# A graph network's kernel: the first layer's own share multiplied out inside the strips that build the adjacency, with the row turns in two banks and another order at the build's end

## The chip, the cores and the metric

The kernel runs on one core of one Trainium2 chip. The metric is the device time of one execution in microseconds (us), lower is better; the kernel before has a median of 1605.82 us over three runs.

## What is computed

The part that matters here is a graph network of five layers on 3125 nodes with 256 channels and 53125 edges. Each layer computes

```python
edge_fea = concatenate([edge_attr[:, 3:] @ ew1[l], edge_attr[:, 0:3] @ ew2[l]])
msg = norm[:, None] * (h[row] + edge_fea)
agg = segment_sum(msg, col)                                   # sum over the edges that end in a node
h = relu(concatenate([h, agg], axis=1) @ mlp_w[l] + mlp_b[l])  # mlp_w[l] is 512 x 256
h = batch_norm(h) over the nodes; relu except after the last layer
```

The first layer's `h` is the layer-normalised input `x`. Since the product with `mlp_w[l]` is over two halves, it splits into `h @ mlp_w[l][:256]`, here called the **own share**, and `agg @ mlp_w[l][256:]`, here called the aggregate's share. After the five layers a mixture-of-experts block follows which the change does not touch.

## The kernel before

**Layout.** `hT` holds `h` transposed, in float32: 128 partitions (channels) x 2 halves x 3125 nodes. Nodes go in 25 tiles of 125 (`NT`, `P`) and in 7 column blocks `COLS` (`NQ`): six of 500 and one of 125. `aggT` is laid out as `hT`. `m` holds the rows of `h` by node, scaled, as two float16 parts. `at` is the adjacency (counts, fp8), 3125 x 3125, so that an aggregate is a dense product of `m` with `at`.

**Aggregation units.** A unit `g` of 0 to 13 is one column block `g // 2` and one channel half `g % 2`. It takes 25 steps (one per source tile) of two matmuls each, then one short matmul for the edge attributes (`attributes`), and then VectorE evicts it to `aggT` (`evict`, line 724). In the first layer units use the PSUM banks 5, 6 and 7 in turn (`FIRST`), so unit `g` waits for the eviction of `g - 3`. All 14 units are 350 steps (`DENSE`).

**The build.** Nothing but the edge list is given, so the first 437 us or so make `at`. Its main loop goes over 63 **strips** `w` of 50 destination nodes. Per strip VectorE makes one-hot tables (lines 1575 to 1582; line 1582 is the last) in one of two buffers (`side = w % 2`), TensorE multiplies them (lines 1817 and 1819, 8 matmuls each), and the buffer is given back. Two strips are a pair `u`: after the odd one TensorE closes the PSUM bank (line 1823), ScalarE copies it out (`encI`, line 1671), VectorE splits it into two groups of nibbles (`low_nibbles`, `high_nibbles`, lines 1545 and 1549, after the strip that is one pair later), and ScalarE writes five tiles of `at` (line 1689). Per ten strips there are also sums of edge attributes: TensorE `turn_sums` (line 1772) in the strips 12, 22, ..., VectorE `attribute_sums` (lines 1561 to 1565) in the next strip, TensorE `turn_rows` (line 1778), ScalarE `rows_out` (line 1664).

**What else runs in the strips.** In strips 0 to 11 TensorE transposes the 25 input tiles (`across`, line 1736) into the four banks 4 to 7 and ScalarE copies each to `hT` (`turned`, line 1644); `across(t)` waits for `turned(t - 4)`. From strip 13 on TensorE also does up to 6 steps of aggregation per strip (`DENSE_W`, line 699), capped by `dense_after` at 50 steps for ten strips, since a block of `at` is complete only every ten strips; the 22nd, 32nd, ... strip has none. 250 steps are done when the loop ends, 100 are left.

**The end of the build.** After strip 62 each engine runs through a list written out by hand, in program order: TensorE turns the last attribute sums and does the 100 steps that are left; VectorE does the nibbles of pairs 30 and 31, both attribute sums, a check sum and the evictions from unit 8 on.

**The first layer's product.** `linear_pe` (line 786) goes over the 7 blocks: 4 matmuls with `hT` (own share) and 4 with `aggT`, all float32, into banks 0 to 3; a profile row counts 2 records for each. ScalarE adds the bias, takes the ReLU and writes `hT` (line 886), and VectorE takes the statistics (`bn_stats`, line 846, then line 849). The next layer starts with 14 matmuls on zeros (line 746), transposes of `hT` (line 680) and its own aggregation (line 690).

The order of the work on each engine is program order, and every wait is a semaphore. The functions and lines that the change touches:

## Time and profile before

| | |
|---|---|
| median of 3 runs (lowest to highest) | 1605.82 us (1603.84 to 1607.27) |
| profiled execution: time / its span | 1611.95 us / 1610.3 us |
| strips 0 to 62 | 170.4 to 438.6 us of the span |
| end of the build | 438.6 to 479.65 us |
| first layer's product | 479.65 to about 522 us |
| busy share of the span, TensorE / VectorE / ScalarE | 88% / 42% / 25% |

The span is the time from the first to the last instruction of the profiled execution. A profile row gives a start, a duration, the engine, the line and the tiles; in square brackets stands the idle time ahead of it on its engine and what ended it.

### The profile page before, as it was taken

To read this page: it belongs to the slowest core of one execution; us is meant where nothing else is said; L and a number is where in the kernel's file an instruction comes from. 1 tells how busy PE (TensorE), PEld (TensorE's weight loads), DVE (VectorE), ACT (ScalarE), POOL (GpSimd) and SP (SyncE) were. 2 spreads that over 40 slices of the span, in tenths; PEclk is the share of its full clock that TensorE was granted. 3 is DMA by queue.
4 is the path that set the end of the run, shared out by engine and by line. 5 is a ranking of instruction groups with operands and counts; after the bars stand their busy time and mean duration, and the time that the engine had idled before them with its cause. 6 is when DMAs were issued, how large, how long until landed. Compare 5 with 4: busy or idle time off the path is not lost.

```text
span 1610.3 us, 25262 instructions
## 1 busy us (share of the span) xinstructions
PE 1421.4 (88%) x9032; PEld 851.9 (53%) x9033; DVE 674.2 (42%) x1562; ACT 399.4 (25%) x1032; POOL 175.5 (11%) x147
## 2 busy tenths in 40 slices
PE   2566589999899999999999999999999873899996
PEld 2555344444444544545445554445445442899995
DVE  7989888887622310122101320023100267333442
ACT  1320354444402400033001420014100240244442
POOL 2000000000000000000000000000000003477774
PEclk9876789999989999999999999999999976999998
DMA  5144000000000000000000000000001383244443
GB/s 124 56 157 161 1 1 2 1 2 1 15 1 0 14 0 1 1 14 0 1 0 1 14 1 0 1 0 15 0 1 46 62 276 96 42 70 69 71 71 44
DMA packets 49545, 57.76 MB, mean 36 GB/s; under 512 B 14320, under 2 KB 41602, under 8 KB 49185
## 3 DMA queue, kind: packets, MB, share of 16 engines
q1 hardware_dynamic: 38688, 41.67, 9.0%
q0 software_dynamic: 10752, 14.69, 5.5%
q8 instruction: 67, 1.10, 0.3%
q14 instruction: 38, 0.30, 0.1%
HBM read 42.36 MB, written 13.99 MB: 35 GB/s over the span
## 4 chain that ended last, share of the span: by engine, by line
PE 80%; DVE 12%; issue 4%; DVEq 2%; ACT 1%; DMA 1%; POOL 1%; SPq 0%; POOLq 0%
PE bank L690 33%; PE bank L786 13%; PE bank L699 10%; PE bank L1214 6%; PE bank L1223 6%; PE bank L1819 3%; DVE ohL L1467 1%; PE bank L680 1%; PE bank L1760 1%; PE bank L705 1%; PE bank L1817 1%; PE bank L1205 1%; PE bank L1180 1%; DVEq L512 1%; PE bank L1742 1%
## 5 line engine op out<-in xcount | busy, mean ns | idle before, releaser
L690 PE MATMUL bank<-at,m 125*128 125x500 fp8e4 (+1 forms) x2800 | 550.9, 351 | 3.5 <-DVE m L647 3.5
L690 PEld LDWEIGHTS bank<-at,m 125*128 125x128 f16 x2800 | 252.4, 97 | 259.8 <-issue 7.1
L724 DVE TENSOR_TENSOR aggT<-bank,dinvB 128x500 f32<-128x500 f32 (+1 forms) x70 | 42.3, 622 | 389.0 <-PE bank L690 355.8
L886 ACT ACTIVATE hT<-bank,prm 128x500 f32<-128x500 f32 (+1 forms) x65 | 42.5, 654 | 569.2 <-PE bank L786 569.2
L699 PE MATMUL bank<-at,m 125*128 125x500 fp8e4 (+1 forms) x700 | 155.4, 376 | 6.8 <-issue 2.5
L935 POOL TENSOR_TENSOR idJ<-idJ,wts 125x1400 f32<-125x1400 f32 x2 | 8.0, 4006 | 1346.0 <-DVE idJ L1093 1346.0
L1214 PEld LDWEIGHTS bank<-xtT,w1c 128*128 128x128 f32 x896 | 111.2, 196 | 2.8
L1214 PE MATMUL bank<-xtT,w1c 128*128 128x128 f32 x896 | 111.4, 279 | 0.0
L786 PE MATMUL bank<-hT,wcur 128*128 128x500 f32 (+1 forms) x280 | 111.1, 539 | 0.0
L786 PE MATMUL bank<-aggT,wcur 128*128 128x500 f32 (+1 forms) x280 | 110.8, 538 | 0.0
L699 PEld LDWEIGHTS bank<-at,m 125*128 125x128 f16 x700 | 63.5, 103 | 83.6 <-issue 33.5
L1223 PE MATMUL bank<-w2s,h1T 128*128 x448 | 106.1, 380 | 0.0
L846 DVE BATCH_NORM_STATS2 zst<-hT 128x6 f32<-128x500 f32 x60 | 40.9, 681 | 153.2 <-ACT hT L886 153.2
L647 DVE SCALAR_TENSOR_TENSOR m<-bank,dinvP,m 125x256 f16<-125x256 f32 x100 | 47.3, 483 | 132.6 <-ACT m L669 132.6
L951 POOL DMA_INDIRECT out_rows<-ytb,rowS x56 | 95.7, 1709 | 53.1 <-issue 23.5
L1689 ACT ACTIVATE at<-encB 125x500 fp8e4<-125x500 uint8 (+1 forms) x96 | 57.5, 599 | 120.7 <-DVE encB L1545 118.1
L1223 PEld LDWEIGHTS bank<-w2s,h1T 128*128 128x128 f32 x448 | 80.8, 190 | 9.2 <-issue 0.2
L786 PEld LDWEIGHTS bank<-aggT,wcur 128*128 128x128 f32 x280 | 50.4, 190 | 55.1 <-issue 55.1
L786 PEld LDWEIGHTS bank<-hT,wcur 128*128 128x128 f32 x280 | 50.1, 190 | 53.4 <-issue 53.2
L1580 DVE TENSOR_TENSOR cnt<-iotaK,nowKD 128x2000 bf16<-128x2000 int16 x63 | 75.2, 1194 | 0.0
L1819 PE MATMUL bank<-cnt,ohS 128*128 128x250 bf16 x504 | 74.3, 293 | 0.0
L1000 ACT ACTIVATE h1T<-bank,b1T 128x128 f32<-128x128 f32 x224 | 64.0, 368 | 25.4 <-issue 20.5
(318 smaller groups left out, 1413.8 us busy)
## 6 DMA issues: line engine op xcount, KB each, us to landing
slrow<-sl_dram SPq DMA_DIRECT2D x26, 512.0 KB, 4.8
...
wraw<-in_L_gnn_mlp_w SPq DMA_DIRECT2D x5, 512.0 KB, 3.5
```

The lines of the kernel that those rows point to most:

```text
L647: dve.scalar_tensor_tensor(m[:, t, 1, :], bank[t % 4][0:P, 0:D], dinvP[:, t:t + 1], m[:, t, 0, :], ALU.mult, ALU.subtract).then_inc(s_lo, 1)
L690: last = pe.matmul(bank[LATER[g % len(LATER)]][:, 0:w], m[:, s, k, h * 128:(h + 1) * 128], at_block(g // H)[:, s, :], start=False, stop=s ...
L699: pe.matmul(bank[FIRST[g % len(FIRST)]][:, 0:w], m[:, s, k, h * 128:(h + 1) * 128], at_block(g // H)[:, s, :], start=s == 0 and k == 0, st ...
L786: last = pe.matmul(bank[2 * (q % 2) + h][:, 0:w], wcur[:, k, h * 128:(h + 1) * 128], rhs, start=k == 0, stop=k == 2 * H - 1)
L886: act.activation(hT[:, h, a:a + w], bank[2 * (q % 2) + h][:, 0:w], ACT.Relu, bias=prm[:, 0, h:h + 1]).then_inc(s_z, 1)
L951: pool.indirect_dma_start(out[:, :], bass.IndirectOffsetOnAxis(ap=rowS[:, j:j + 1], axis=0), ytb[:, j % XB, :], None, compute_op=ALU.add). ...
L1000: last = act.activation(h1T[:, u, k, :], bank[4 + u][:, k * TT:(k + 1) * TT], ACT.Relu, bias=b1T[:, bass.ds(e, 1), k:k + 1].rearrange("p a ...
L1214: last = pe.matmul(bank[4 + u][:, k * TT:(k + 1) * TT], w1c[:, u, h, k * 128:(k + 1) * 128], xtT[:, u, h, :], start=h == 0, stop=h == H - 1)
L1223: last = pe.matmul(bank[6 + u][:, 0:D], h1T[:, u, k, :], w2s[:, bass.ds(e, 1), k, :].rearrange("p a f -> p (a f)"), start=k == 0, stop=k = ...
L1580: dve.tensor_tensor(cnt1[side][:, :, :, :], to_all(iotaK[:, :, :], U // 2), by_pairs(nowKD[:, side, 0, :], GW), ALU.is_equal)
L1689: last = act.activation(at_block(q)[:, field:field + FIELDS * (GROUPS - 1) + 1:FIELDS, a:a + n], byte[:, f, :, 0:n], ACT.Copy, saturate=False,
L1819: last = pe.matmul(out_w, ohS[side][:, j // 2, :, j % 2], cnt1[side][:, j // 2, :, j % 2].rearrange("p (g n) -> p g n", g=GROUPS), start=F ...
```

## The change

It does the following.

1. **Own share in the strips.** The upper half of the first layer's weights is loaded early into `w1z`, and its bias into `biasz`, by two DMAs on SyncE's queue ahead of its wait for the end of the loop. In the even strips 4 to 16 TensorE computes `own_share(q)` for block `q = w / 2 - 2` (4 float32 matmuls into banks 6 and 7), and ScalarE writes the result, scaled and with the bias, over `hT` (in pair `u = q + 2`). `own_share(q)` waits until ScalarE has written block `q - 1`; aggregation unit 1, which uses bank 6, waits for all of them.
2. **Row turns.** `across` uses the two banks 4 and 5 instead of four, so that `across(t)` waits for `turned(t - 2)`; strip 0 does 2 tiles and strip 1 does 3, instead of 3 and 2.
3. **First layer's product.** Only the aggregate's 4 matmuls per block are left. VectorE adds `hT` to their result (`add_own`, 14 additions, one block ahead of the statistics), ScalarE takes the ReLU from and to `hT`, and TensorE waits for VectorE's additions instead of ScalarE's.
4. **End of the build.** TensorE does 6 steps of aggregation ahead of `turn_rows(5)`, and 19 instead of 25 behind `turn_sums(6)`. VectorE does `attribute_sums(5)` and the evictions of units 8 and 9 between the nibbles of pairs 30 and 31. ScalarE does `rows_out(5)` before it writes the tiles of pair 31.

```diff
@@ -774,16 +782,16 @@

-        def linear_pe(pe, base, following):
+        def linear_pe(pe, base, following, first=0):
             pe.wait_ge(s_wc, base(1) + 1)
...
                 if q >= 2:
-                    pe.wait_ge(s_z, base(ZC) + H * (q - 1))
-                for k in range(2 * H):
+                    pe.wait_ge(s_ad, H * (q - 1)) if first else pe.wait_ge(s_z, base(ZC) + H * (q - 1))
+                for k in range(first, 2 * H):
                     rhs = (hT if k < H else aggT)[:, k % H, a:a + w]
                     for h in range(H):
-                        last = pe.matmul(bank[2 * (q % 2) + h][:, 0:w], wcur[:, k, h * 128:(h + 1) * 128], rhs, start=k == 0, stop=k == 2 * H - 1)
+                        last = pe.matmul(bank[2 * (q % 2) + h][:, 0:w], wcur[:, k, h * 128:(h + 1) * 128], rhs, start=k == first, stop=k == 2 * H - 1)
                         if k == 2 * H - 1:
@@ -833,10 +841,24 @@
                 attribute_parts(dve, step, lambda: dve.tensor_tensor(ewS[:, :, :], ewT[:, :, :], cfi[:, 1, :].bitcast(F32).unsqueeze(2).to_broadcast([128, H, 4]), ALU.mult))
+            def add_own(q):
+                a, w = COLS[q]
+                for h in range(H):
+                    dve.wait_ge(s_mlp, H * q + h + 1)
+                    dve.tensor_tensor(hT[:, h, a:a + w], bank[2 * (q % 2) + h][:, 0:w], hT[:, h, a:a + w], ALU.add).then_inc(s_ad, 1)
+
+            if first_layer:
+                add_own(0)
             for q, (a, w) in enumerate(COLS):
+                if first_layer and q + 1 < NQ:
+                    add_own(q + 1)
                 if q == NQ - 1:
-                    dve.wait_ge(s_mlp, base(H * NQ) + H * NQ)
-                    step(dve.tensor_scalar(hT[:, 1, a:a + w], bank[2 * (q % 2) + 1][:, 0:w], prm[:, 0, 1:2], 0.0, ALU.add, ALU.max))
+                    if first_layer:
+                        dve.wait_ge(s_ad, H * NQ)
+                        step(dve.tensor_scalar(hT[:, 1, a:a + w], hT[:, 1, a:a + w], 0.0, None, ALU.max))
+                    else:
+                        dve.wait_ge(s_mlp, base(H * NQ) + H * NQ)
+                        step(dve.tensor_scalar(hT[:, 1, a:a + w], bank[2 * (q % 2) + 1][:, 0:w], prm[:, 0, 1:2], 0.0, ALU.add, ALU.max))
                     step(dve.bn_stats(zst[:, 1, q, :], hT[:, 1, a:a + w]))
@@ -879,11 +901,15 @@

-        def linear_act(act, base, following):
+        def linear_act(act, base, following, first_layer):
             for q, (a, w) in enumerate(COLS):
                 for h in range(H if q < NQ - 1 else 1):
-                    act.wait_ge(s_mlp, base(H * NQ) + H * q + h + 1)
-                    act.activation(hT[:, h, a:a + w], bank[2 * (q % 2) + h][:, 0:w], ACT.Relu, bias=prm[:, 0, h:h + 1]).then_inc(s_z, 1)
+                    if first_layer:
+                        act.wait_ge(s_ad, H * q + h + 1)
+                        act.activation(hT[:, h, a:a + w], hT[:, h, a:a + w], ACT.Relu).then_inc(s_z, 1)
+                    else:
+                        act.wait_ge(s_mlp, base(H * NQ) + H * q + h + 1)
+                        act.activation(hT[:, h, a:a + w], bank[2 * (q % 2) + h][:, 0:w], ACT.Relu, bias=prm[:, 0, h:h + 1]).then_inc(s_z, 1)
                 if following and q == NQ - 2:
@@ -1280,6 +1306,10 @@

+            sp.wait_ge(s_ds, NLB)
+            sp.dma_start(w1z[:, :, :], mlp_w[0:1, 0:D, :].rearrange("a (k p) c -> p (a k) c", p=128)).then_inc(s_wz, 16)
+            with nc.allow_non_contiguous_dma(reason="a few values for each channel"):
+                sp.dma_start(biasz[:, :], mlp_b[0:1, :].rearrange("a (h p) -> p (a h)", p=128)).then_inc(s_wz, 16)
             sp.wait_ge(s_cnt, PAIRS)
@@ -1593,14 +1623,18 @@
             assert NW % 2
-            for u in range(PAIRS - 2, PAIRS):
-                low_nibbles(u)
-                high_nibbles(u)
+            low_nibbles(PAIRS - 2)
+            high_nibbles(PAIRS - 2)
             attribute_sums(NQ - 2)
+            dve.wait_ge(s_cnt, PAIRS)
+            for g in range(evicted, H * NQ - 2 * H):
+                evict(dve, zero, g, FIRST)
+            low_nibbles(PAIRS - 1)
+            high_nibbles(PAIRS - 1)
             attribute_sums(NQ - 1)
...
             dve.tensor_reduce(bad[:, :], sums[:, :], axis=XYZ, op=ALU.add).then_inc(s_flagp, 1)
-            for g in range(evicted, H * NQ - H):
+            for g in range(H * NQ - 2 * H, H * NQ - H):
                 evict(dve, zero, g, FIRST)
@@ -1641,7 +1675,7 @@
                 act.wait_ge(s_xT, t + 1)
-                act.activation(hT[:, :, t * P:(t + 1) * P], bank[4 + t % 4][:, 0:H * P].rearrange("p (h n) -> p h n", h=H), ACT.Copy).then_inc(s_xTe, 1)
+                act.activation(hT[:, :, t * P:(t + 1) * P], bank[4 + t % 2][:, 0:H * P].rearrange("p (h n) -> p h n", h=H), ACT.Copy).then_inc(s_xTe, 1)

@@ -1674,8 +1708,15 @@
                     turned(t)
+                if 2 <= u < NQ + 2:
+                    a, w = COLS[u - 2]
+                    act.wait_ge(s_pz, u - 1)
+                    for h in range(H):
+                        act.activation(hT[:, h, a:a + w], OWN[h][:, 0:w], ACT.Identity, scale=2.0 ** -H0_EXP, bias=biasz[:, h:h + 1]).then_inc(s_hz, 1)
                 if SB < 2 * u + 1 < NW and (2 * u + 1) % SB == 5:
                     rows_out((2 * u + 1) // SB - 1)
+                if u == PAIRS - 1:
+                    rows_out(NQ - 2)
                 a = PW * u
@@ -1690,13 +1731,12 @@
                 last.then_inc(s_at, 1)
-            for b in range(NQ - 2, NQ):
-                rows_out(b)
+            rows_out(NQ - 1)
             for l in range(L):
...
                     m_rows_act(act, base, normalise_act(act, prev, False))
-                linear_act(act, base, following if l + 1 < L else None)
+                linear_act(act, base, following if l + 1 < L else None, not l)
             last = normalise_act(act, layer(L - 1), True)
@@ -1728,12 +1768,10 @@
             def across(t):
-                if t == 3:
-                    pe.wait_ge(s_ewm, 1)
-                if t >= 4:
-                    pe.wait_ge(s_xTe, t - 3)
+                if t >= 2:
+                    pe.wait_ge(s_xTe, t - 1)
                 for h in range(H):
-                    last = pe.transpose(bank[4 + t % 4][:, h * P:(h + 1) * P], xin[:, t, h * 128:(h + 1) * 128], ident[0:P, 0:P])
+                    last = pe.transpose(bank[4 + t % 2][:, h * P:(h + 1) * P], xin[:, t, h * 128:(h + 1) * 128], ident[0:P, 0:P])
                 last.then_inc(s_xT, 1)
@@ -1765,6 +1803,19 @@

+            def own_share(q):
+                a, w = COLS[q]
+                pe.wait_ge(s_xTe, min((q + 1) * BT, NT))
+                if q == 0:
+                    pe.wait_ge(s_wz, 32)
+                    pe.wait_ge(s_ewm, 1)
+                else:
+                    pe.wait_ge(s_hz, H * q)
+                for k in range(H):
+                    for h in range(H):
+                        last = pe.matmul(OWN[h][:, 0:w], w1z[:, k, h * 128:(h + 1) * 128], hT[:, k, a:a + w], start=k == 0, stop=k == H - 1)
+                last.then_inc(s_pz, 1)
+
             def turn_sums(b):
@@ -1788,6 +1839,8 @@
                         pe.wait_ge(s_at, min(CQ // PW * (g // H + 1), PAIRS))
+                        if g == 1:
+                            pe.wait_ge(s_hz, H * NQ)
                         if g >= len(FIRST):
@@ -1825,8 +1878,10 @@
                     ahead = turns(pe, w + 1), turns_before(pe, w + 1)
-                for t in range(2 * w + (w > 0), min(2 * w + 3, NT)):
+                for t in range(2 * w + (w > 1), min(2 * w + 2 + (w > 0), NT)):
                     across(t)
+                if w >= 4 and w % 2 == 0 and w // 2 - 2 < NQ:
+                    own_share(w // 2 - 2)
                 if w > SB and w % SB == 2:
@@ -1834,10 +1889,11 @@
                 done = dense_to(dense_after(w))
+            done = dense_to(min(done + DENSE_W, DENSE))
             turn_rows(NQ - 2)
...
             turn_sums(NQ - 1)
-            done = dense_to(min(done + NT, DENSE))
+            done = dense_to(min(done + NT - DENSE_W, DENSE))
             turn_rows(NQ - 1)
...
```

The last hunks give `linear_pe`, `statistics_dve` and `linear_act` a flag that is true for the first layer; the path for other inputs, which this run does not take, gets it too.

Where instructions now stand, by engine. Names in the rows: `xin` the normalised input, `ident` the identity, `w1z` the early weights, `ohD`, `ohS` and `cnt` the one-hot tables, `s4r` and `s4h` the attribute sums. First TensorE in strips 4 and 5; before, the transposes of strip 4 (line 1736) are followed at once by strip 5:

```order
L1736 MATMUL bank<-ident,xin 128x125 x4
L1813 UNCONDITIONAL_BRANCH
L1813 ISA
L1817 MATMUL bank<-ohD_90,now 12x50 x8
L1819 MATMUL bank<-cnt_1_102,ohS_92 128x5x50 x8
```

The same place of TensorE in the changed kernel, where lines 1774, 1870 and 1872 are the lines 1736, 1817 and 1819 of before:

```order
L1774 MATMUL bank<-ident,xin 128x125 x4
L1816 MATMUL bank<-hT,w1z 128x500 x4
L1866 UNCONDITIONAL_BRANCH
L1866 ISA
L1870 MATMUL bank<-ohD_91,now 12x50 x8
L1872 MATMUL bank<-cnt_1_104,ohS_93 128x5x50 x8
```

The own share stands between the transposes of the even strip and the odd strip's matmuls; six such places follow, two strips apart.

TensorE behind strip 62, before, with the semaphores that each row waits for:

```order
L1825 MATMUL bank<-zeros 12x1
L1772 MATMUL bank<-ident,s4r 125x12 [waits s_s4Te,s_s4r]
L1772 MATMUL bank<-ident,s4r 125x12 x3
L1778 MATMUL bank<-negI,s4h 36x125 [waits s_s4K]
L1778 MATMUL bank<-negI,s4h 36x125 x3
L699 MATMUL bank<-at,m 128x500 [waits s_agge,s_at]
L699 MATMUL bank<-at,m 128x500 x49
L705 MATMUL bank<-s4T,ewm 128x500 [waits s_s4Te]
```

The same place in the changed kernel:

```order
L1878 MATMUL bank<-zeros 12x1
L1823 MATMUL bank<-ident,s4r 125x12 [waits s_s4Te,s_s4r]
L1823 MATMUL bank<-ident,s4r 125x12 x3
L707 MATMUL bank<-at,m 128x500 [waits s_agge,s_at]
L707 MATMUL bank<-at,m 128x500 x11
L1829 MATMUL bank<-negI,s4h 36x125 [waits s_s4K]
L1829 MATMUL bank<-negI,s4h 36x125 x3
L707 MATMUL bank<-at,m 128x500 x38
L713 MATMUL bank<-s4T,ewm 128x500 [waits s_s4Te]
```

Twelve matmuls of unit 10 have moved ahead of the row that waits for VectorE's `s4h`.

VectorE behind the last strip, before, from the nibbles of pair 30 on:

```order
L1545 TENSOR_SCALAR encB<-encI 125x500 [waits s_at,s_enc]
L1549 TENSOR_SCALAR encI<-encI 125x500 [waits s_nib]
L1545 TENSOR_SCALAR encB<-encI 125x500 [waits s_at,s_enc]
L1549 TENSOR_SCALAR encI<-encI 125x500 [waits s_nib]
L1561 TENSOR_REDUCE s4P<-bank 125x16 [waits s_s4t]
```

And in the changed kernel, where lines 1575, 1579, 1591 to 1595 and 732 are 1545, 1549, 1561 to 1565 and 724 of before:

```order
L1575 TENSOR_SCALAR encB<-encI 125x500 [waits s_at,s_enc]
L1579 TENSOR_SCALAR encI<-encI 125x500 [waits s_nib]
L1591 TENSOR_REDUCE s4P<-bank 125x16 [waits s_s4t]
L1593 CAST s4h<-s4P 125x12x4 [waits s_dv]
L1594 TENSOR_TENSOR s4P<-s4P,s4h 125x16 [waits s_dv]
L1593 CAST s4h<-s4P 125x12x4 [waits s_dv]
L1594 TENSOR_TENSOR s4P<-s4P,s4h 125x16 [waits s_dv]
L1595 CAST s4h<-s4P 125x12x4 [waits s_dv]
L732 TENSOR_TENSOR aggT<-bank,dinvB 128x500 [waits s_agg,s_cnt]
L732 TENSOR_TENSOR aggT<-bank,dinvB 128x500 [waits s_agg]
L1575 TENSOR_SCALAR encB<-encI 125x500 [waits s_at,s_enc]
L1579 TENSOR_SCALAR encI<-encI 125x500 [waits s_nib]
```

The attribute sums and two evictions now stand ahead of the second pair of nibbles.

## Rows read from the trace of the kernel before

**Rows 1.** Windows: stretch, its length, busy time (count) by engine, granted clock, DMA

```profile
199.90:215.20 15.30, 10.45 (x86) 7.15 (x87) 13.58 (x28) 9.80 (x33) 0.00 (x0) 0.86 0.01 2
479.60:521.00 41.40, 41.40 (x107) 19.21 (x106) 10.57 (x29) 8.26 (x13) 0.00 (x0) 1.00 0.00 0
```

**Rows 2.** Timeline, strips 3 to 5: start, duration, engine, line, [idle before]

```profile
180.73 0.36 PE L1817 MATMUL bank<-ohD,now 128*12 128x50 bf16 x8 [1.22 <-DVE ohS L1582]
...
184.17 0.56 ACT L1671 ACTIVATE encI<-bank 125x500 int32<-125x500 f32 x1
184.63 1.17 ACT L1644 ACTIVATE hT<-bank 128x250 f32<-128x250 f32 x4
184.67 0.36 PE L1817 MATMUL bank<-ohD,now 128*12 128x50 bf16 x8 [1.47 <-DVE ohS L1582]
186.28 0.65 PE L1736 MATMUL bank<-ident,xin 125*128 125x125 f32 x4 [0.24 <-issue]
188.12 0.37 PE L1817 MATMUL bank<-ohD,now 128*12 128x50 bf16 x8 [1.19 <-DVE ohS L1582]
```

**Rows 3.** Timeline of TensorE, strips 13 to 15

```profile
218.65 0.49 PE L1817 MATMUL bank<-ohD,now 128*12 128x50 bf16 x8 [1.15 <-DVE ohS L1582]
220.79 4.66 PE L699 MATMUL bank<-at,m 125*128 125x500 fp8e4 x12
225.59 0.39 PE L1817 MATMUL bank<-ohD,now 128*12 128x50 bf16 x8
227.11 2.71 PE L699 MATMUL bank<-at,m 125*128 125x500 fp8e4 x12
229.75 0.39 PE L1817 MATMUL bank<-ohD,now 128*12 128x50 bf16 x8
```

**Rows 4.** Timeline, strips 17 and 21 to 23

```profile
239.94 0.16 PE L1823 MATMUL bank<-zeros 128*128 128x1 bf16 x1
240.17 0.59 ACT L1671 ACTIVATE encI<-bank 125x500 int32<-125x500 f32 x1 [1.26 <-PE bank L1823]
...
259.38 0.68 DVE L724 TENSOR_TENSOR aggT<-bank,dinvB 128x500 f32<-128x500 f32 x1 [2.44 <-PE bank L705]
263.10 0.49 PE L1817 MATMUL bank<-ohD,now 128*12 128x50 bf16 x8 [1.21 <-DVE ohS L1582]
```

**Rows 5.** Timeline, end of the build

```profile
438.55 0.60 PE L1772 MATMUL bank<-ident,s4r 12*125 12x12 f32 x4
442.21 0.42 DVE L1545 TENSOR_SCALAR encB<-encI 125x500 int32<-125x500 int32 x1 [5.28 <-ACT encI L1671]
444.35 0.60 PE L1778 MATMUL bank<-negI,s4h 125*36 125x125 bf16 x4 [5.20 <-DVE s4h L1565]
444.88 13.29 PE L699 MATMUL bank<-at,m 125*128 125x500 fp8e4 x50
460.86 12.14 PE L699 MATMUL bank<-at,m 125*128 125x500 fp8e4 x50 [2.17 <-DVE aggT L724]
```

**Rows 6.** Timeline, first layer's product: second block, last block, statistics

```profile
486.46 3.52 PE L786 MATMUL bank<-hT,wcur 128*128 128x500 f32 x8
486.67 0.68 ACT L886 ACTIVATE hT<-bank,prm 128x500 f32<-128x500 f32 x1 [0.16 <-PE bank L786]
487.38 0.68 DVE L846 BATCH_NORM_STATS2 zst<-hT 128x6 f32<-128x500 f32 x1 [0.16 <-ACT hT L886]
489.82 3.52 PE L786 MATMUL bank<-aggT,wcur 128*128 128x500 f32 x8
521.11 1.06 PE L786 MATMUL bank<-aggT,wcur 128*128 128x125 f32 x8
523.35 0.55 DVE L849 BATCH_NORM_AGGREGATE zmv<-zst 128x2 f32<-128x42 f32 x2
```

**Rows 7.** Timeline of TensorE, start of the second layer

```profile
526.80 0.67 PE L680 MATMUL bank<-ident,hT 128*125 128x128 f32 x4 [0.60 <-DVE hT L644]
```

**Rows 8.** Page, part 6: DMA issues, KB each, median us to landing

```profile
wraw<-in_L_gnn_mlp_w SPq DMA_DIRECT2D x5, 512.0 KB, 3.5
```

18 lines of the change are left out of this document (13 added, 5 removed).

## The prediction

> **What bounds the kernel now.** I read first the windows over the first 530 us, since the change acts nowhere else; then the timelines of the strips, of the build's end and of the first layer's product, always asking which wait ends last. They show three regimes.
>
> In strips 0 to 12 VectorE sets the pace: every strip on TensorE starts right behind VectorE's last one-hot (line 1582) after 1.2 to 1.5 us of idle time [rows 2], and in one stretch of 15.3 us VectorE is busy 13.6 and TensorE 10.5 us [rows 1]. Two strips take 7.6 us: strip 5 starts at 188.12 and strip 13 at 218.65, so 30.5 us for four pairs [rows 2, 3]. TensorE has about 2.4 us to spare per strip.
>
> From strip 13 on TensorE sets it. Strips follow each other without idle time [rows 3], until the 22nd, where VectorE has to wait 2.44 us for TensorE's last unit before it evicts, and TensorE then waits 1.21 us for the one-hots behind that eviction [rows 4]. So a delay of TensorE in strips 13 to 21 is not absorbed in strip 22: the eviction, the one-hots and strip 23 all shift with it.
>
> At the end of the build TensorE idles 5.20 us for VectorE's `s4h`, which stands behind the nibbles of pair 31, which wait for ScalarE; and 2.17 us for an eviction that stands behind the last attribute sums. Both times it then runs at the lower clock for a while [rows 5]. Then comes the first layer's product, where TensorE is busy all 41.4 us [rows 1].
>
> **The first layer's product.** For a block of 500, the own share takes from 486.46 to 489.82, so 3.36 us [rows 6]; six of them are 20.2 us, and the block of 125 takes 1.06 less the overlap of its records, about 0.9 us. That is 21.0 us off TensorE. What is left per block is 3.36 us on TensorE. VectorE now has two additions, priced by the eviction of the same shape at 0.68 us [rows 4], and two statistics of 0.68 us [rows 6], 2.7 us in all: less than 3.36, so TensorE stays the bound, and if each wait cost VectorE 0.15 us more it would have 3.3, still not more. Only the tail gets longer. Before, the statistics of the whole sixth block were done while TensorE worked on the seventh, and line 849 starts 1.2 us behind its end (521.11 + 1.06 = 522.17, 523.35) [rows 6]. Now VectorE does, from the sixth block's end on: an addition, the statistics of the fifth block (1.4), the two short additions (0.7), those of the sixth (1.4), and a short ReLU and two short statistics (1.1), some 5.2 us, of which TensorE's last block covers 1.1. So line 849 starts 4.1 us behind TensorE's end, 2.9 us later than before. **Sum: -18.1 us** (bounds -21.0, if the tail were free, and -16).
>
> **The next layer's start.** Its TensorE idles 0.60 us before the first transposes [rows 7]; with the longer tail that becomes some 3 us. After 2.17 and 5.20 us of idle time the trace shows the lower clock [rows 5]. A spell of it costs 2.65 us where strips 13 and 14 show it: strip 13 takes 6.94 us, strip 14 with the same work 4.16, and 0.1 to 0.2 us of the difference is closing and clearing a bank; most of the rest is in the 12 matmuls of line 699, 4.66 against 2.71 us [rows 3]. I take **+1.5 us**, between nothing and 2.7.
>
> **The end of the build.** TensorE now has 12 matmuls (2.7 us) between its turned sums and the row that needs `s4h`, and VectorE makes `s4h` before the nibbles of pair 31. Its nibbles of pair 30 wait for nothing that comes after strip 61, so its six small operations follow TensorE's turned sums at 439.15 (438.55 + 0.60); they take 1.3 us (from the end of the second nibbles, 442.21 + 2 x 0.42, to 444.35) [rows 5] and end near 440.6, while TensorE's twelve end near 441.8: no wait. Evictions 8 and 9 follow at once, so unit 11 finds its bank free, and unit 12, too. What goes is 5.20 + 2.17 us of idle time and the lower clock: 50 matmuls at strip 14's rate (12 from 227.11 to the next strip at 229.75, 2.64 us with the loop's 0.1) are about 10.5 us, and took 13.29 and 12.14 [rows 3, 5], so 2.8 and 1.6 us. **Sum: -11.5 us** (bounds -7.4, the two waits alone, and -11.8). The extra evictions and `rows_out(5)` stand beside these matmuls; without that cover they would cost 1.4 and 0.6 us.
>
> **Strips 0 to 12.** Here is the price. The own share is 3.36 us on TensorE in every second strip, more than the idle time of one strip, and the two banks for the row turns add a wait. In an odd strip the transposes of two tiles now need the first two copies of the same pair by ScalarE. In strip 3 ScalarE is still writing `at` and comes to its first copy at 184.63, 3.9 us after the strip's start [rows 2]. Two copies (0.6), a transpose and the start of the next strip (0.6 and 0.3) put strip 4 at 186.0 instead of 184.67. Its matmuls and transposes take 2.26 us (184.67 to 186.93), the own share 3.36, the loop 0.2: strip 5 starts at 191.8 instead of 188.12, **+3.7 us**. From then on TensorE and ScalarE set the pace in turn. From the start S of an odd strip: its bank closes at S + 1.3, ScalarE's `encI` starts 0.23 later [rows 4], its first copy 0.46 behind that, and two take 0.6 [rows 2]; the second tile's transposes end at S + 3.05, the even strip starts at S + 3.4, its matmuls and transposes end at S + 5.7, and the own share and the loop at S + 9.3. ScalarE's two new writes (0.68 each, as line 886) are done by S + 4.9 and are not waited for. So a pair takes 9.3 us instead of 7.6; four pairs and 0.5 us for the attribute sums' bank are **+7.1 us**, and strip 13 starts 10.8 us later. The bounds are 0, if the own share fitted into the idle time, and 4 x 3.4 + 3.7 = 17, if none did.
>
> **Strips 13 to 22.** Own shares 5 and 6 come on top of full strips: 3.36 and 0.9 us with 0.3 of loop. Unit 1 waits in strip 17 until ScalarE has written the last own share: after line 1823 at 239.94 it starts `encI` at 240.17 [rows 4], then two short writes, some 0.6 us behind the moment at which TensorE comes there. Against this, own share 4 in strip 12 keeps TensorE busy, and strip 13 may run at the full clock: -2.65 us [rows 3]. **Sum: +2.5 us**. The later cycles are as before.
>
> **The clock in the strips.** The wait in strip 3 grows to 2.9 us, ahead of strip 4 and the first own share; that is like the 2.17 us after which the trace shows the lower clock [rows 5]. I count one spell there and half of another in the four pairs, at 2.65 us each: **+4.0 us**. In the old strips the clock averages 0.86 [rows 1], but there TensorE waited anyway and a spell cost nothing; now it does. The Trainium skill (TensorE: Matmul & The Clock Gate, "A second HAM failure mode: psum-queue depth-cycling") tells of a kernel that cycled through its PSUM banks with small idle times, where the clock went up and down and throughput fell. It speaks against the two-bank turns; what that would do here is the second rival below. The two DMAs for `w1z` and `biasz` are issued before the strips begin, 512 KB of such weights land in 3.5 us [rows 8], and strip 4 is 14 us into the loop: nothing.
>
> **Sum.** -18.1 + 1.5 - 11.5 + 10.8 + 2.5 + 4.0 = -10.8 us. The profiled execution, 1611.95 us, would be at 1601.1. Its time is 0.4% above the median of the runs; taken off that median, 1605.8 - 10.8 = **1595 us**.
>
> **Rivals.**
>
> - *The own share hides.* If VectorE still set the pace through strip 12, the +10.8 and the +4.0 would vanish: 1580 us. For it speaks 2.4 us of idle time per strip, 4.8 in a pair; against it, that the own share stands in one strip and cannot be split, and that the row turns add their wait. Chance 0.08.
> - *The lower clock in each pair.* A pair now has about 1.2 us of idle time behind the odd strip's matmuls and is short of work around it. If each of the four pairs has a spell, the clock costs 5 x 2.65 = 13.3 instead of 4.0 us: 1604.5 us, no change to be told. For it speaks that strip 23 comes behind only 1.21 us of idle time, as strip 13 behind 1.15 us [rows 3, 4]. Against it, that the own share makes TensorE busier than it was. Chance 0.10.
> - *The build's end gives half.* VectorE's list is in order, and the evictions now stand ahead of the last nibbles; if unit 12 then waits for `at`, or unit 10 for an eviction, only the 5.20 us and little else go: 1601 us. Against it, unit 12 starts some 20 us after the twelve matmuls of unit 10, and ScalarE is then long through with `at`. Chance 0.12.
> - *Slower: the lower clock throughout strips 3 to 12.* At half the clock a pair's own share is 6.7 instead of 3.4 us, its matmuls and transposes 2.7 us more: 6.1 us for each of five pairs, 30 instead of the 4.0 us: 1621 us. It decides from 15 us of clock cost on, more than five spells. Against it, the clock already averages 0.86 with less work there [rows 1]. Chance 0.05.
>
> My forecast has 0.65.
>
> **How the numbers follow.** The likeliest case reaches from 1587 (no spell, next layer's start free, a shorter pair) to 1602 (one more spell and a few tenths more per pair). That takes in the rival at 1601, and leaves out 1580, 1604.5, 1621 and the edges of the likeliest: 0.2 in all. 0.2% of this time is 3.2 us, about what a measurement can tell from no change. Slower than 1609 are the last rival and a point from others, 0.06; within it are most of the second rival and a little of the first case, 0.11; the rest, 0.83, is faster.
>
> **What the profile would show.** The own share's groups have 3.4 us in the even strips 4 to 16, and strip 5 starts near 192 to 194; strip 13 near 230 to 234, instead of 218.65; strip 23 some 15 to 18 us later than 263.1. If strip 13 starts by 222, the first rival holds; if line 1817's 8 matmuls take 0.49 instead of 0.36 us [rows 2, 3] in most even strips, the second. From strip 62 to the product TensorE has no wait over 1 us and takes about 29.5 instead of 41.1 us. The product takes near 21 us on TensorE with no idle time in it; if it has idle time behind VectorE, my price for the additions is wrong. The row ahead of the next layer's transposes shows about 3 us of idle time. The forecast fails most easily in the pair's 9.3 us, which is counted out of pieces that stand apart in the trace of before.

## The result

| | changed | before | ratio [95% interval] |
|---|---|---|---|
| median (lowest to highest) | 1591.22 us (1590.09 to 1593.06) | 1605.81 us (1603.84 to 1607.27) | 0.9911 [0.9898, 0.9924] |
| profiled execution / its span | 1591.85 us / 1590.2 us | 1611.95 us / 1610.3 us | |
| TensorE's mean granted clock | 0.945 | 0.939 | |

The change makes the kernel 14.6 us faster; 10.8 were forecast. Run once more (`a1_changed_again`, below), it gave a ratio of 0.9903 [0.9886, 0.9920].

The profile of the changed kernel, read in the same order. First the windows: strips 3 and 4, 5 to 12, 13 to 22, the end of the build behind strip 62's matmuls, the product up to the next layer's first transposes, and those with the matmuls behind them. Columns: stretch, length, busy time and count of TensorE, its weight loads, VectorE, ScalarE and GpSimd, granted clock, DMA share and GB/s.

```profile
178.60:190.40 11.80, 8.84 (x51) 5.24 (x52) 10.51 (x22) 7.98 (x25) 0.00 (x0) 0.86 0.01 2
190.40:225.90 35.50, 30.59 (x203) 17.59 (x202) 24.13 (x50) 24.61 (x69) 0.00 (x0) 1.00 0.00 1
225.90:272.90 47.00, 43.56 (x299) 23.22 (x299) 35.28 (x76) 19.13 (x53) 0.00 (x0) 0.99 0.00 1
445.60:475.30 29.70, 29.70 (x219) 16.51 (x217) 7.03 (x25) 5.98 (x24) 0.00 (x0) 1.00 0.09 19
475.30:503.50 28.20, 25.64 (x77) 11.78 (x76) 22.04 (x62) 9.16 (x17) 0.00 (x0) 1.00 0.00 0
503.50:509.20 5.70, 4.80 (x16) 2.67 (x17) 0.90 (x3) 2.51 (x7) 0.00 (x0) 0.57 0.42 94
```

Strips 5 to 12 of the kernel before, which the prediction's rows did not cover as a whole, in the same view:

```profile
188.10:218.60 30.50, 20.73 (x170) 14.25 (x170) 27.08 (x56) 19.09 (x61) 0.00 (x0) 0.82 0.01 2
```

VectorE was busy 27.08 of 30.50 us there and TensorE 20.73; now it is TensorE with 30.59 of 35.50. The bound has changed sides, as the prediction said. But TensorE's clock went from 0.82 to 1.00, and its busy time rose by 9.9 us for 13.4 us of added own share (4 x 3.36).

TensorE's timeline through strips 3 to 7, 13, 17 and 23, beside [rows 2 to 4] (line 1774 are the row turns, 1816 the own share, and each row of line 1870 starts a strip):

```profile
178.63 0.36 PE L1870 MATMUL bank<-ohD,now 128*12 128x50 bf16 x8 [0.29 <-DVE ohS L1612]
...
182.95 0.78 PE L1774 MATMUL bank<-ident,xin 125*128 125x125 f32 x4 [2.93 <-ACT hT L1678]
...
184.07 0.51 PE L1870 MATMUL bank<-ohD,now 128*12 128x50 bf16 x8
184.51 1.85 PE L1872 MATMUL bank<-cnt,ohS 128*128 128x250 bf16 x8
...
186.93 3.52 PE L1816 MATMUL bank<-hT,w1z 128*128 128x500 f32 x8
190.38 0.39 PE L1870 MATMUL bank<-ohD,now 128*12 128x50 bf16 x8
...
192.75 0.71 PE L1774 MATMUL bank<-ident,xin 125*128 125x125 f32 x4 [0.98 <-ACT hT L1678]
...
193.60 0.38 PE L1870 MATMUL bank<-ohD,now 128*12 128x50 bf16 x8
...
195.69 3.52 PE L1816 MATMUL bank<-hT,w1z 128*128 128x500 f32 x8
199.14 0.39 PE L1870 MATMUL bank<-ohD,now 128*12 128x50 bf16 x8
...
225.90 0.39 PE L1870 MATMUL bank<-ohD,now 128*12 128x50 bf16 x8
...
227.46 2.71 PE L707 MATMUL bank<-at,m 125*128 125x500 fp8e4 x12 [0.15 <-issue]
...
251.10 2.27 PE L707 MATMUL bank<-at,m 125*128 125x500 fp8e4 x10 [0.23 <-ACT hT L1715]
...
272.93 0.49 PE L1870 MATMUL bank<-ohD,now 128*12 128x50 bf16 x8 [1.26 <-DVE ohS L1612]
```

From strip 5 on a pair takes 8.76 us (190.38 to 199.14), and the only wait in it is the 0.98 us for ScalarE's copies (line 1678) behind the two-bank turns. Strip 5 starts 11.75 us behind strip 3 (before 7.39), strip 13 35.52 behind strip 5 (30.53), strip 23 47.03 behind strip 13 (44.45).

The end of the build, beside [rows 5]:

```profile
445.67 0.60 PE L1823 MATMUL bank<-ident,s4r 12*125 12x12 f32 x4
446.20 2.71 PE L707 MATMUL bank<-at,m 125*128 125x500 fp8e4 x12
...
449.17 8.21 PE L707 MATMUL bank<-at,m 125*128 125x500 fp8e4 x38
...
475.34 20.39 PE L794 MATMUL bank<-aggT,wcur 128*128 128x500 f32 x48
495.79 1.05 PE L794 MATMUL bank<-aggT,wcur 128*128 128x125 f32 x8
...
503.53 0.67 PE L688 MATMUL bank<-ident,hT 128*125 128x128 f32 x4 [2.00 <-DVE hT L652]
505.07 3.52 PE L698 MATMUL bank<-at,m 125*128 125x500 fp8e4 x8 [0.87 <-DVE m L655]
```

No wait stands between strip 62 and the product: both idle times (5.20 and 2.17 us) are gone, and 50 matmuls (2.71 + 8.21 us) run at the full clock. From the first of these rows to the product are 29.7 us (41.1 before). The product's six blocks take 20.39 us in one run of 48 records, without a wait for VectorE's additions. Behind it VectorE has a longer tail:

```profile
495.77 0.68 DVE L848 TENSOR_TENSOR hT<-bank,hT 128x500 f32<-128x500 f32 x1 [0.16 <-PE bank L794]
...
496.36 1.25 DVE L868 BATCH_NORM_STATS2 zst<-hT 128x6 f32<-128x500 f32 x2
...
500.08 0.55 DVE L871 BATCH_NORM_AGGREGATE zmv<-zst 128x2 f32<-128x42 f32 x2
```

Line 871 (849 of before) starts 3.24 us behind TensorE's end (495.79 + 1.05 = 496.84). TensorE then idles 2.00 us before the next layer's transposes, and over these transposes and the 8 aggregation matmuls behind them the granted clock is 0.57.

### The profile page after: what moved, and what is told of

The parts are those of the page before. It is cut to its first block, busy times and chain, and to the rows that moved or that the text cites. A ratio compares the mean times of both kernels' runs of the same rounds, so it can differ in the third digit from the quotient of the medians.

```text
span 1590.2 us, 25301 instructions
## 1 busy us (share of the span) xinstructions
PE 1411.2 (89%) x9032; PEld 847.0 (53%) x9033; DVE 681.1 (43%) x1576; ACT 406.8 (26%) x1046; POOL 175.8 (11%) x147
## 4 chain that ended last, share of the span: by engine, by line
PE 81%; DVE 12%; issue 3%; ACT 1%; DVEq 1%; DMA 1%; POOL 1%; SPq 0%; POOLq 0%
PE bank L698 34%; PE bank L794 12%; PE bank L707 9%; PE bank L1240 6%; PE bank L1249 6%; PE bank L1872 3%; DVE ohL L1497 1%; PE bank L688 1%; PE bank L1798 1%; PE bank L1816 1%; PE bank L1870 1%; PE bank L713 1%; PE bank L1231 1%; PE bank L1206 1%; PE bank L1780 1%
## 5 line engine op out<-in xcount | busy, mean ns | idle before, releaser
L912 ACT ACTIVATE hT<-bank,prm 128x500 f32<-128x500 f32 (+1 forms) x52 | 34.0, 654 | 529.4 <-PE bank L794 529.4
L794 PE MATMUL bank<-hT,wcur 128*128 128x500 f32 (+1 forms) x224 | 88.8, 539 | 0.0
L677 ACT ACTIVATE m<-bank,dinvP 125x256 f16<-125x256 f32 x100 | 46.2, 474 | 97.9 <-PE bank L688 97.1
```

Source lines behind the costliest of these rows:

```text
L677: act.activation(m[:, t, 0, :], bank[t % 4][0:P, 0:D], ACT.Copy, scale=dinvP[:, t:t + 1]).then_inc(s_hi, 1)
L794: last = pe.matmul(bank[2 * (q % 2) + h][:, 0:w], wcur[:, k, h * 128:(h + 1) * 128], rhs, start=k == first, stop=k == 2 * H - 1)
```

## The experiments

The medians, each against the kernel before on the same chip:

| run | what it is | median (us) | before | ratio [95% interval] |
|---|---|---|---|---|
| `e1_end_only` | before, with part 4 alone | 1596.43 | 1605.57 | 0.9949 [0.9936, 0.9963] |
| `e2_old_end` | changed, without part 4 | 1600.51 | 1605.57 | 0.9968 [0.9959, 0.9977] |
| `e3_turns_only` | before, with part 2 alone | 1604.74 | 1605.57 | 0.9998 [0.9989, 1.0007] |
| `e4_warm` | changed, 24 zero matmuls for 14 | 1591.19 | 1605.57 | 0.9912 [0.9897, 0.9927] |
| `e4b_warm_again` | the same once more | 1590.92 | 1608.07 | 0.9896 [0.9878, 0.9913] |
| `e5_copies_first` | changed, ScalarE's copies earlier | 1586.09 | 1606.15 | 0.9874 [0.9859, 0.9889] |
| `e6_half_share` | changed, half of the own share left out (one execution) | 1586.49 | 1606.15 | |
| `e7_both` | `e5` with 24 zero matmuls | 1585.74 | 1608.07 | 0.9861 [0.9842, 0.9881] |
| `e8_five_blocks` | changed, own share of five blocks | 1587.95 | 1606.15 | 0.9888 [0.9873, 0.9903] |
| `e9_five_and_first` | `e5` and `e8` together | 1581.65 | 1606.15 | 0.9842 [0.9827, 0.9857] |
| `a1_changed_again` | the changed kernel | 1591.98 | 1608.07 | 0.9903 [0.9886, 0.9920] |

Runs with the same time of before shared a chip. Where a run is set against the changed kernel's 1591.22 us below, the chips differ; by the distance to before on each chip, the gains of `e5`, `e8` and `e9` would be 5.5, 3.6 and 9.9 us instead of 5.1, 3.3 and 9.6.

**The end of the build alone** (`e1_end_only`), in the kernel before:

```diff
-            for u in range(PAIRS - 2, PAIRS):
-                low_nibbles(u)
-                high_nibbles(u)
+            low_nibbles(PAIRS - 2)
+            high_nibbles(PAIRS - 2)
             attribute_sums(NQ - 2)
+            dve.wait_ge(s_cnt, PAIRS)
+            for g in range(evicted, H * NQ - 2 * H):
+                evict(dve, zero, g, FIRST)
+            low_nibbles(PAIRS - 1)
+            high_nibbles(PAIRS - 1)
...
+            done = dense_to(min(done + DENSE_W, DENSE))
             turn_rows(NQ - 2)
```

and the edits that belong to it: 19 steps instead of 25 behind `turn_sums(6)`, the last evictions' range, and the two of `rows_out`.

> The kernel before with part 4 of the change alone (the order at the build's end). My theory: the end of the build is worth what its two waits and the two spells at the lower clock cost, 11.4 us, whatever the strips do, so about 1594.4 us against 1605.8; TensorE from the end of strip 62 to the first layer's product takes near 29.7 instead of 41.1 us. Rival (the parts need each other, for example because the earlier end only helps once the product is shorter): under 6 us, above 1600.

Measured: 9.1 us less. Its rows behind strip 62, with the first of the product:

```profile
434.31 2.71 PE L699 MATMUL bank<-at,m 125*128 125x500 fp8e4 x12
...
437.28 8.21 PE L699 MATMUL bank<-at,m 125*128 125x500 fp8e4 x38
...
463.44 3.62 PE L786 MATMUL bank<-hT,wcur 128*128 128x500 f32 x8
```

Strip 62 starts at 432.35, so the end takes 31.09 us, as in the changed kernel (444.24 to 475.34, 31.10). The waits go as forecast and the rival (under 6 us) falls, but 2.3 us of the forecast gain are missing.

**The changed kernel with the old end** (`e2_old_end`): the edit above and its two companions undone.

> The changed kernel with the old order at the build's end, so parts 1 to 3 alone. My theory: the strips give back 12 us of the 19 that the product saves, less 3 us at the next layer's start: 3 to 4 us faster than before, so about 1602.5 us. Rival (the strips' loss is noise in the profiled execution, or is absorbed later): 12 us or more faster, below 1594.

Measured: 5.1 us less than before, so parts 1 to 3 bring 5.1 and part 4 brings 9.1; together 14.2 of the 14.6 us. The parts add up. (3 to 4 us were expected of parts 1 to 3.) The rows tell where `e1`'s missing 2.3 us are:

```profile
452.93 0.61 PE L1824 MATMUL bank<-negI,s4h 125*36 125x125 bf16 x4 [5.19 <-DVE s4h L1595]
453.47 12.17 PE L707 MATMUL bank<-at,m 125*128 125x500 fp8e4 x50
...
468.33 10.73 PE L707 MATMUL bank<-at,m 125*128 125x500 fp8e4 x50 [2.17 <-DVE aggT L732]
```

The two idle times are those of [rows 5] to a hundredth, but 50 matmuls take 12.17 us behind the first and 10.73 behind the second, where [rows 5] have 13.29 and 12.14. The lower clock behind a wait of the same length is not the same in every execution. The old end takes 40.01 us here (strip 62 at 445.71, product at 485.72), 40.32 in `e3`, and 42.52 in the profile of before: 31.10 is 8.9 and 9.2 us less than the first two.

**The row turns alone** (`e3_turns_only`), in the kernel before:

```diff
-                if t >= 4:
-                    pe.wait_ge(s_xTe, t - 3)
+                if t >= 2:
+                    pe.wait_ge(s_xTe, t - 1)
...
-                    last = pe.transpose(bank[4 + t % 4][:, h * P:(h + 1) * P], xin[:, t, h * 128:(h + 1) * 128], ident[0:P, 0:P])
+                    last = pe.transpose(bank[4 + t % 2][:, h * P:(h + 1) * P], xin[:, t, h * 128:(h + 1) * 128], ident[0:P, 0:P])
```

with ScalarE's copies from the same two banks and the tiles of strips 0 and 1 dealt out as in the change.

> The kernel before with part 2 alone: the row turns in two banks. My theory: the new wait of TensorE for ScalarE's copies (0.98 us in an odd strip, 2.93 us in strip 3) lies in the idle time that VectorE's pace leaves, but for about 1 us in strip 3, so within 1.5 us of 1605.8. Rival (the two-bank turns are what slows the strips, by wait and by the lower clock): 5 us slower or more, above 1610.

Measured: no difference, 0.9998 [0.9989, 1.0007]. The waits are there all the same:

```profile
181.69 0.36 PE L1815 MATMUL bank<-ohD,now 128*12 128x50 bf16 x8 [0.72 <-DVE ohS L1582]
...
186.01 1.09 PE L1734 MATMUL bank<-ident,xin 125*128 125x125 f32 x4 [2.94 <-ACT hT L1644]
...
193.81 0.70 PE L1734 MATMUL bank<-ident,xin 125*128 125x125 f32 x4 [1.16 <-ACT hT L1644]
```

and its windows over strips 3 and 4 and over strips 5 to 12:

```profile
181.70:190.50 8.80, 5.86 (x42) 4.08 (x42) 7.71 (x18) 5.48 (x17) 0.00 (x0) 0.72 0.00 1
190.50:219.90 29.40, 20.43 (x172) 14.00 (x172) 26.08 (x54) 19.06 (x61) 0.00 (x0) 0.85 0.01 1
```

TensorE waits 2.94 us in strip 3 and 1.16 us in strip 5. Strips 3 and 4 take 8.8 us instead of 7.4 (180.73 to 188.12 before), partly since the clock falls behind the long wait: 0.72 over these two strips, where the window of the same strips of before (180.70 to 188.10) has 1.00. The eight strips behind them then wait less for VectorE and take 29.4 us instead of 30.5, at a granted clock of 0.85 (before 0.82). Over all ten strips the two kernels are 0.3 us apart (38.2 and 37.9). The prediction weighed a rule of the Trainium skill here (TensorE: Matmul & The Clock Gate, "A second HAM failure mode: psum-queue depth-cycling"). For the turns of strips 5 to 12 the trace does not agree with it: two banks in turn, with short waits, do not bring the clock down there; the one drop stands behind a single long wait.

**ScalarE's copies earlier** (`e5_copies_first`). In the changed kernel ScalarE comes to the even strip's two copies only behind its wait for the nibbles and its writes of `at`; this lets it do all of them when the transposes land:

```diff
-                for t in range(4 * u + (u > 0), min(4 * u + 5, NT)):
+                for t in range(4 * u + 3 if u else 0, min(4 * u + 5, NT)):
                     turned(t)
...
+                for t in range(4 * u + 5, min(4 * u + 7, NT)):
+                    turned(t)
                 a = PW * u
```

> The changed kernel, with ScalarE's copies of the even strip's two tiles moved ahead of the odd strip's end: it makes them before it waits for the nibbles, so that the odd strip's transposes find their banks free. My theory: the 2.93 us in strip 3 and the 0.98 us in each odd strip are this wait and lie on the path. Strips 3 to 5 take near 9 instead of 11.75 us and strips 5 to 13 near 31.5 instead of 35.52 us (VectorE's pace of 30.5 is the floor), so about 6 us less, 1585.5. Rival (the own share itself is what sets the pace, and the wait only fills time that TensorE would lose anyway): strips 5 to 13 stay above 34.5 us, and the time within 2 us of 1591.

Measured: 1586.09 us, 5.1 less than the changed kernel. TensorE in strips 3 to 7:

```profile
181.29 0.36 PE L1872 MATMUL bank<-ohD,now 128*12 128x50 bf16 x8 [0.85 <-DVE ohS L1612]
...
182.91 0.64 PE L1776 MATMUL bank<-ident,xin 125*128 125x125 f32 x4 [0.23 <-issue]
...
190.78 0.39 PE L1872 MATMUL bank<-ohD,now 128*12 128x50 bf16 x8
...
198.81 0.39 PE L1872 MATMUL bank<-ohD,now 128*12 128x50 bf16 x8
```

Both waits are gone: in strip 5, too, only 0.30 us of issue stands ahead of the transposes. Strip 5 comes 9.49 us behind strip 3 (11.75 in the changed kernel), a pair takes 8.03 us instead of 8.76, and strip 13 comes at 222.52, 31.74 behind strip 5 (35.52). The sum of the two is 6.0 us less in the profile, as expected, and the rival (strips 5 to 13 stay above 34.5 us) falls. So the turns' wait, which costs nothing alone (`e3`), costs 5 to 6 us beside the own share, with the lower clock in strip 4 that went with it. (`e7`, with the same edit, takes 4.9 us less than the changed kernel for these ten strips in its profile.)

**Half of the own share** (`e6_half_share`), in the changed kernel with its old copies; the kernel leaves out the second half of the own share:

```diff
-                for k in range(H):
+                for k in range(1):
```

> The changed kernel with only half of the own share's matmuls in the strips (k = 0 alone, so the first layer leaves out half of its own share). My theory: a pair takes 8.75 us because TensorE's work and its wait add up; 1.68 us less of work gives 7.1, below VectorE's 7.6, so strips 5 to 13 take 30.5 to 31.5 us and the own share is hidden there. Rival (the two-bank wait sets the pace whatever TensorE has to do): above 34 us.

Measured: 1586.49 us in one execution. Its window over strips 5 to 12:

```profile
192.00:222.60 30.60, 25.18 (x187) 15.55 (x186) 25.72 (x52) 24.52 (x72) 0.00 (x0) 0.94 0.00 1
```

Strips 5 to 12 take 30.7 us (191.98 to 222.65), as in the kernel before: half a share hides in VectorE's pace even with the two-bank wait in place, and the second half costs 4.9 us of its 6.7 (4 x 1.68) there. With strips 3 and 4 (10.0 us instead of 11.75) it is 6.6 us.

**The own share of five blocks only** (`e8_five_blocks`): blocks 5 and 6 keep all 8 matmuls in the product, ScalarE and VectorE treat them as before, and strips 14 and 16 have no own share.

```diff
+OWNQ = 5
...
+                begin = first if q < OWNQ else 0
+                for k in range(begin, 2 * H):
...
-                if w >= 4 and w % 2 == 0 and w // 2 - 2 < NQ:
+                if w >= 4 and w % 2 == 0 and w // 2 - 2 < OWNQ:
                     own_share(w // 2 - 2)
```

> The changed kernel with the own share in the strips for blocks 0 to 4 only; blocks 5 and 6 are computed whole in the product, and ScalarE evicts them as before. My theory: blocks 5 and 6 gain nothing in strips 14 and 16, where TensorE is the bound, and they make VectorE's tail. Product: TensorE 4.2 us more, line of the batch statistics' end 1.2 instead of 3.2 us behind it, next layer without the spell at the lower clock (3.0); strips 13 to 23 take 43.3 to 44.2 instead of 47.0 us. In all 4 to 5 us less, near 1587. Rival (VectorE's tail is made by the whole chain of additions, not by the last blocks): tail and idle time stay, and the time is 1591 or above.

Measured: 1587.95 us (1587.06 to 1589.14), 3.3 less than the changed kernel (4 to 5 were expected). The intervals of the two ratios touch, but none of the changed kernel's ten executions is below 1590.09. Strips 13 to 22 take 42.44 us (227.00 to 269.44) instead of 47.03, so leaving out 4.2 us of own share gave 4.6. The product costs 2.2 us more (472.73 to 503.11, 30.38, against 28.19), and VectorE's tail is shorter, as its last row shows, 1.2 us behind TensorE's end (before, too, 1.2), so the rival falls:

```profile
497.42 1.06 PE L796 MATMUL bank<-aggT,wcur 128*128 128x125 f32 x8
...
499.66 0.55 DVE L870 BATCH_NORM_AGGREGATE zmv<-zst 128x2 f32<-128x42 f32 x2
```

TensorE then idles 0.60 us before the next transposes, as before, and no lower clock follows.

**Both** (`e9_five_and_first`): the edits of `e5` and `e8`.

> Both edits, copies first and five blocks only. If the two losses lie in different places of the path they add: 10 to 11 us less than the changed kernel, near 1581. If they overlap, near 1585.

Measured: 1581.65 us (1578.12 to 1583.49), 9.6 us less than the changed kernel and the best of all: the two gains (5.1 and 3.3) add, where 10 to 11 us were expected and 6 if they overlapped. Over strips 5 to 12 (191.90 to 223.60 us) TensorE is busy 30.39 of 31.70 us, at a granted clock of 1.00: next to nothing is left to fill in these strips.

**The next layer's start** (`e4_warm`, `e4b_warm_again`, `e7_both`): 24 instead of 14 matmuls on zeros while TensorE waits for the second layer's first rows, in the changed kernel twice and in `e5` once.

```diff
-            for n in range(WARM):
+            for n in range(WARM + (10 if warmer else 0)):
```

> The changed kernel with 24 instead of 14 matmuls on zeros ahead of the second layer, so that TensorE is busy some 2.2 us longer and idles near 0 instead of 2.00 us before the first transposes. My theory: the lower clock there comes from the idle time; with it gone the first 8 matmuls of line 698 take 1.85 instead of 3.52 us, and the time falls by 2.5 to 3 us to about 1588.5. Rival (the clock falls for another reason, for example in the transposes themselves): no change, or 0.3 us slower if the added matmuls reach into the wait.

> The 24 matmuls on zeros once more. In the profile they took 3.0 us off the stretch from the product to the second layer's rows, and nothing was to be seen in the timed runs. My theory: the 3 us are real and were lost in the scatter of the stretches outside: 1588.3 us here. Rival: the timed runs don't have the spell at the lower clock there, so the edit is worth nothing: 1591 us.

> ScalarE's copies first (as in the run of that edit alone, 1586.1 us) and the 24 matmuls on zeros. If the matmuls are worth 3 us: 1583 us; if they are worth nothing in timed runs: 1586 us.

In the profile of `e4_warm` the idle time is filled and the lower clock gone:

```profile
501.16 5.29 PE L754 MATMUL bank<-zeros 128*128 128x500 bf16 x24
506.32 0.67 PE L688 MATMUL bank<-ident,hT 128*125 128x128 f32 x4
507.86 1.86 PE L698 MATMUL bank<-at,m 125*128 125x500 fp8e4 x8 [0.87 <-DVE m L655]
```

The 8 matmuls take 1.86 us instead of 3.52. The times say less than the 2.5 to 3 us that the theory had: 1591.19 and 1590.92 against the changed kernel's 1591.22 and 1591.98, and 1585.74 against `e5`'s 1586.09. That is 0 to 1.1 us, with the executions of one kernel 3 to 5 us apart (the ratio of `e7` is 0.0013 below that of `e5`, 2 us, well inside both intervals). What the lower clock costs there on the average stays open, between nothing and about 2 us by these pairs.

**The changed kernel again** (`a1_changed_again`), on the chip of `e4b` and `e7`:

> The changed kernel once more, beside the next two on the same chip: 1591.2 us within 1 us.

Measured: 1591.98 us, as expected. Its start of the second layer:

```profile
504.74 0.67 PE L688 MATMUL bank<-ident,hT 128*125 128x128 f32 x4 [2.01 <-DVE hT L652]
506.28 3.52 PE L698 MATMUL bank<-at,m 125*128 125x500 fp8e4 x8 [0.87 <-DVE m L655]
```

The same 3.52 us again, but over a shorter stretch: the fifth transposes come 12.76 us behind the first, where the profile above has 14.05 and an execution with no lower clock there (`e4`) 11.08. And `e6`, whose wait is the same, shows no lower clock at all:

```profile
497.16 0.67 PE L688 MATMUL bank<-ident,hT 128*125 128x128 f32 x4 [2.02 <-DVE hT L652]
498.70 1.86 PE L698 MATMUL bank<-at,m 125*128 125x500 fp8e4 x8 [0.87 <-DVE m L655]
```

All the profiles together:

| profiles | idle before the transposes (us) | first 8 matmuls (us) | fifth transposes behind the first (us) |
|---|---|---|---|
| changed | 2.00 | 3.52 | 14.05 |
| `e2` | 2.00 | 3.51 | 13.93 |
| `a1` | 2.01 | 3.52 | 12.76 |
| `e5` | 2.02 | 2.68 | 12.76 |
| `e6` | 2.02 | 1.86 | 11.09 |
| before, `e1`, `e3`, `e8`, `e9` | 0.59 to 0.60 | 1.86 | 11.09 |
| `e4`, `e4b`, `e7` | 0 | 1.86 | 11.08 to 11.09 |

So a wait of 2 us costs between 0 and 3.0 us behind it, 1.8 on the average of five profiles, and without it there was no lower clock in eight.

## Why the prediction was right, and where its sizes were off

Changes between the two profiles, taken at the start of the strips' first matmuls, add up to 20.3 us; the two spans are 20.1 us apart:

| stretch on TensorE | before | changed | change | forecast |
|---|---|---|---|---|
| up to strip 3 | 180.73 | 178.63 | -2.1 | 0 |
| strips 3 and 4 | 7.39 | 11.75 | +4.4 | +3.7, and 1 of the clock's 1.5 spells (2.65) |
| strips 5 to 12 | 30.53 | 35.52 | +5.0 | +7.1, and half a spell (1.35) |
| strips 13 to 22 | 44.45 | 47.03 | +2.6 | +2.5 |
| strips 23 to 61 | 174.03 | 171.31 | -2.7 | 0 |
| strip 62 to the product | 42.52 | 31.10 | -11.4 | -11.5 |
| product to the next layer | 47.15 | 28.19 | -19.0 | -18.1 |
| next layer's first to fifth transposes | 11.09 | 14.05 | +3.0 | +1.5 |

The first and fifth rows are no effect of the change. The strips' start lies anywhere between 168.5 and 172.1 us in these profiles, and strips 23 to 61 take 170.3 us in `e1` and 170.4 in `e3`, which do not touch them either. What differs are the strips 33, 43 and 53, which take 1.5, 1.2 and 0.8 us more in the profile of before, by longer spells at the lower clock (granted clock over strips 23 to 61: 0.92, and 0.96 in the changed kernel). In strip 33 of the kernel before:

```profile
307.49 0.49 PE L1817 MATMUL bank<-ohD,now 128*12 128x50 bf16 x8 [1.26 <-DVE ohS L1582]
...
309.62 4.61 PE L699 MATMUL bank<-at,m 125*128 125x500 fp8e4 x12
```

and of the changed one:

```profile
317.40 0.36 PE L1870 MATMUL bank<-ohD,now 128*12 128x50 bf16 x8 [1.20 <-DVE ohS L1612]
...
319.13 2.70 PE L707 MATMUL bank<-at,m 125*128 125x500 fp8e4 x12 [0.35 <-issue]
```

Nearly the same wait (1.26 and 1.20 us) ahead of the same work, and 1.9 us of difference in the twelve matmuls alone. That is why the profiles are 20.1 us apart and the medians 14.6: the profiled execution of before had more time in such spells than the others, here (the other twelve profiles take 170.1 to 172.2 us for strips 23 to 61) and at the build's end.

- **The product** (-18.1). Right. TensorE stays the bound, VectorE's additions take 0.68 us and keep up. The tail was 3.24 us and not 4.1: records that follow each other overlap. From the last block's additions on, two statistics take 1.17 us to the next instruction (496.36 to 497.53, and 497.91 to 499.08) and not 1.4, twice, and the two short additions 0.38 us and not 0.7.
- **The next layer's start** (+1.5). The place is right: 2.00 us of idle time and a lower clock behind it, +3.0, +2.8, +1.7, +1.7 and 0 us in five profiles with this wait, and 0 with more zero matmuls. Timed, the term cannot be told from nothing.
- **The end of the build** (-11.5). The mechanism is right, `e1` shows it alone. The size is that of the profiled execution of before; of the medians it is -9.1. The mis-sized part is the 4.4 us for the lower clock (2.8 and 1.6), of which `e2` and `e3` show 1.4 and 1.8 behind the first wait and nothing behind the second. The bounds given (-7.4 to -11.8) hold it.
- **Strips 0 to 12** (+10.8, and +4.0 for the clock). This was the term most off: measured +9.4 for both, so 5.4 us less. The order of events in a pair was right, the wait for ScalarE's two copies among them, but the pair takes 8.76 us and not 9.3. The even strip starts 3.22 us behind the odd one (193.60 - 190.38; forecast 3.4), its matmuls and transposes take 2.09 (forecast 2.3), own share and loop 3.45 (forecast 3.6): all three were sums of records that overlap by a tenth or two. In strip 4 there was a short spell (1.85 instead of 1.08 us for line 1872, gone by the own share), worth some 0.8 us (from strip 4's start to its own share 2.86 us, in strip 6 2.09), and none in the pairs.
- **Strips 13 to 22** (+2.5). Right, with the pieces foreseen: strip 13 at the full clock (2.71 instead of 4.66 us), unit 1 waiting for the last own share, with 0.23 us and not 0.6.
- **The rivals.** "The own share hides" falls: strip 13 starts 7.25 us later than before (9.4 us, counted from the start of strip 3). It needed half the work (`e6`), and removing the wait comes near it: in `e5` strips 5 to 12 take 1.2 us more than before. The prediction gave this rival twice the room that there was: it has 2.4 us of idle time per strip and 4.8 in a pair, but [rows 1] cover four strips with 4.85 us of it, so 1.2 in a strip and 2.4 in a pair. By that room the own share, 3.36 us in a pair, would have cost about 3.7 us in four pairs (an estimate: 4 x (3.36 - 2.43), from [rows 1] and [rows 6]); that `e5` shows 1.2 goes with its granted clock of 1.00 instead of 0.82, at which TensorE's busy time rose by 9.6 us (30.37 against 20.73) for 13.4 added. "The lower clock in each pair" and "throughout strips 3 to 12" fall with the granted clock of 1.00. "The build's end gives half" falls with `e1`. The last rival's price was right, but not the point from which it decides: 1609 is 14 us above the forecast, which already has 4.0 us for the clock, so it takes 18 us of clock cost and not 15.
- **The signs.** Three of the times named were missed: strip 5 starts at 190.38 (192 to 194 were given), strip 13 at 225.90 (230 to 234), strip 23 at 272.93, 9.8 us later than before (15 to 18). All are early, by the strips' start, which is 1.9 us earlier in this profile, and by the strips' cost, which is up to 5.4 us below the forecast. The product (21.5 us on TensorE without idle time) and the build's end (29.7 us) came as said; the idle time before the next layer was 2.0 us and not 3.

In sum: the strips came 5.4 us cheaper than forecast and the product gave 0.9 more, the end of the build gave 2.4 less by the medians, together 3.9 us, about the 3.8 by which the time is below the forecast. This takes the first two terms from profiles and leaves the next layer's start out. The medians alone say it more plainly. Parts 1 to 3 were forecast at -18.1 + 1.5 + 10.8 + 2.5 + 4.0 = +0.7 us, a slight loss, and `e2` has them at -5.1; part 4 was forecast at -11.5, and `e1` has it at -9.1. So the mechanisms were right, but that the total is within 4 us is in part luck: errors of 5.8 and 2.4 us point opposite ways.

The prediction had the two-bank wait in its pair of strips, but did not ask what it costs by itself. `e3` and `e5` show that: alone nothing, beside the own share 5 to 6 us. The 9.4 us that strips 3 to 12 lost are not one cost of the own share and another of the wait, side by side: taking away the wait gives back 6.0 us in the profile (`e5`), taking away half of the own share 6.6 (`e6`). And `e8` shows that two of the seven own shares were better left where they were: in strips 14 and 16 TensorE has no idle time, so moving them gains nothing and lengthens VectorE's tail.
